# A fused window-attention, global-attention and expert kernel on one core: closing products in the ring of first scores, the last chunk's scores on full columns, token norm sums on GpSimd

## The reference

```
x: [16, 56, 56, 32] f32
x = x + window_attention_block(group_norm(x))   # 7x7 windows, 4 heads, MLP
t = x as tokens                                 # [16, 3136, 32]
n = layer_norm(t)                               # over the 32 channels
q, k, v = n Wq + bq, n Wk + bk, n Wv + bv
t = t + (softmax(q k^T / sqrt(32)) v + n)       # one head, 3136 x 3136 scores per image
n = layer_norm(t)
t = t + experts(n)   # 16 experts: each takes its 8 best tokens of an image, pools
                     # them, two small layers, result added to those tokens
```

## Time and profile before

| | |
|---|---|
| median of 3 runs | 2749.19 us (2747.32 to 2753.39) |
| the profiled execution's own time | 2750.07 us |
| its span, first to last instruction | 2748.3 us |
| TensorE matmuls busy | 2550.2 us, 93% |
| VectorE busy | 2308.6 us, 84% |
| ScalarE busy | 2111.2 us, 77% |
| GpSimd busy | 621.9 us, 23% |
| mean granted TensorE clock | 0.969 of full speed |

### The profile page before, as it was taken

How to read it: one execution, slowest core, us unless ns; L and a number is a source line. 1 busy time by engine, 2 the same in 40 slices (tenths; PEclk the granted TensorE clock), 3 DMA queues, 4 the chain that set the end, 5 groups by cost and what they waited for, 6 DMA issues and landing times.

```text
span 2748.3 us, 118778 instructions
## 1 busy us (share of the span) xinstructions
PE 2550.2 (93%) x54353; PEld 1772.0 (64%) x54353; DVE 2308.6 (84%) x2944; ACT 2111.2 (77%) x3927; POOL 621.9 (23%) x506
## 2 busy tenths in 40 slices
PE   4899999999698999999999999999999999999987
PEld 3455555555343777777777777777777776777756
DVE  5799999999457988889889888898898888988943
ACT  4688888888643888788888887888888877878872
POOL 0566666666400101101101011011010110110100
PEclk6899999999897999999999999999999999999997
DMA  4000000000165010110110101101101011010003
GB/s 103 8 20 26 20 20 25 20 26 20 64 267 124 3 27 3 27 27 3 27 27 4 27 3 27 27 3 27 27 3 27 4 26 27 3 27 3 3 2 95
DMA packets 92807, 85.93 MB, mean 31 GB/s; under 512 B 61108, under 2 KB 82197, under 8 KB 91285
## 3 DMA queue, kind: packets, MB, share of 16 engines
q1 hardware_dynamic: 92085, 78.29, 10.8%
q10 hardware_dynamic: 224, 0.07, 0.0%
HBM read 39.60 MB, written 32.11 MB: 26 GB/s over the span
## 4 chain that ended last, share of the span: by engine, by line
PE 75%; ACT 11%; DVE 8%; issue 4%; SPq 1%; DMA 1%; POOL 0%; POOLq 0%; DVEq 0%; ACTq 0%
PE ps L1711 18%; PE ps L1696 17%; PE ps L1668 16%; ACT arena L911 5%; PE ps L1496 3%; DVE arena L1159 3%; PE ps L1774 2%; DVE arena L1271 2%; PE ps L1515 2%; PE ps L1488 2%; PE ps L1506 2%; PE ps L1527 2%; ACT arena L743 1%; PE ps L1543 1%; PE ps L1566 1%
## 5 line engine op out<-in xcount | busy, mean ns | idle before, releaser
L1271 DVE TENSOR_REDUCE arena<-ps 128x2 f32<-128x896 f32 (+1 forms) x1408 | 1485.8, 1082 | 193.7 <-PE ps L1668 189.4
L911 ACT ACTIVATE arena<-ps 128x512 f32<-128x512 f32 (+1 forms) x2464 | 1351.2, 597 | 310.0 <-PE ps L1696 299.8
L1696 PE MATMUL ps<-arena 97*32 97x512 f16 x10976 | 1104.1, 354 | 11.1 <-issue 6.7
L1711 PE MATMUL ps<-arena 128*32 128x128 f32 x19200 | 1009.3, 273 | 27.9 <-ACT arena L911 19.4
L1668 PE MATMUL ps<-arena 96*32 96x448 f16 x10976 | 885.6, 356 | 18.6 <-DVE arena L1261 8.9
L1711 PEld LDWEIGHTS ps<-arena 128*32 128x32 f32 x19200 | 702.9, 110 | 226.5 <-ACT arena L911 67.3
L1668 PEld LDWEIGHTS ps<-arena 96*32 96x32 f16 x10976 | 381.5, 97 | 178.0 <-DVE arena L1271 85.9
L1696 PEld LDWEIGHTS ps<-arena 97*32 97x32 f16 x10976 | 394.1, 95 | 40.5 <-ACT arena L911 11.5
L640 POOL TENSOR_TENSOR tok<-arena,tok 128x128 f32<-128x128 f32 (+1 forms) x112 | 48.0, 428 | 1359.6 <-DVE arena L1293 1357.7
L585 POOL TENSOR_TENSOR arena<-arena 113x784 f32<-113x784 f32 x128 | 192.7, 1505 | 156.5 <-DVE arena L1135 156.5
L580 POOL TENSOR_TENSOR arena<-arena 113x784 f32<-113x784 f32 x128 | 192.6, 1505 | 86.8 <-DVE arena L1124 86.8
(11 more groups left out here) (188 smaller groups left out, 2457.4 us busy)
## 6 DMA issues: line engine op xcount, KB each, us to landing
arena<-qk_scratch SPq DMA_DIRECT2D x96, 196.0 KB, 4.0
qk_scratch<-arena SPq DMA_DIRECT2D x16, 512.0 KB, 4.4
arena<-ximg SPq DMA_DIRECT2D x16, 400.0 KB, 7.1
arena<-in_x SPq DMA_DIRECT2D x4, 1568.0 KB, 10.9
xa_scratch<-arena SPq DMA_DIRECT2D x32, 196.0 KB, 1.9
res_scratch<-arena SPq DMA_DIRECT2D x32, 196.0 KB, 2.0
arena<-xa_scratch SPq DMA_DIRECT2D x4, 1568.0 KB, 8.3
arena<-res_scratch SPq DMA_DIRECT2D x4, 1568.0 KB, 11.0
```

Source lines behind the costliest of these rows:

```text
L911: act.activation(pk[0:rows, k % DEPTH, QC * m:QC * m + n], ps[0:rows, w % SB, 0:n], ACT.Exp, scale=float(C) ** -0.5).then_inc(att["exp"], 1)
L1271: dve.tensor_reduce(mxp[0:rows, p, 2 * u:2 * u + k], ps[0:rows, at_:at_ + k, 0:KN], AX_X, ALU.max)\
L1696: last = pe.matmul(ps[r:r + 32, bank, at_ % QC:at_ % QC + chunk_cols(c)], k2[p][0:97, T * t + r:T * t + r + 32], q2[p][0:97, QC * c:QC * c ...
L1711: last = pe.matmul(ps[C * g:C * (g + 1), AVB, 0:T], vf[p][:, t, :], pk[:, x % DEPTH, at_ + T * g:at_ + T * (g + 1)], start=(t == 0), stop= ...
```

## The change

Five things are done; the new orders follow from the tables.

1. The closing product no longer writes to bank 3 but takes a slot of the ring of first scores. A table `ring_no` numbers all uses of the ring, pairs and closing products, in TensorE's order; a use waits until the one two before it has been consumed (`ring_free`). VectorE's product of a closing counts `ring` as a maximum does, and VectorE works the slots off in the same order.
2. The first key sums of a chunk wait for ScalarE's copy (`acopy`), and no longer for VectorE. Nothing is held back a step: COPY_LAG is 2, the copy stands between the two exponentials of its step, and the sums of a chunk's first step come behind the closing product. Steps 53 to 56 become

The diff, cut to its core:

```diff
-        SUMS_LAG, COPY_LAG, OUT_LAG, WEIGHTED_LAG = 2, 3, 3, 4
-
-        def sums_step(x):
-
-            return x + SUMS_LAG + int(x in first_of)
+        SUMS_LAG, COPY_LAG, OUT_LAG = 2, 2, 3
 
         def sums_at(k, place):
 
-            found = [(x, late) for late in (1, 0) for x in range(NSTEP) if sums_step(x) - NSTEP * late == k]
-            end, both = scores_of[k], len(found) > 1
-            tiles = [(x, late, i) for x, late in found for i in range(len(steps2[x][1]) if steps2[x][0] < NQ - 1 else 1)]
-            return [m for n, m in enumerate(tiles) if place == (end if both or n else min(1, end))]
+            x, late = (k - SUMS_LAG) % NSTEP, int(k < SUMS_LAG)
+            c, tiles, _ = steps2[x]
+            places = [scores_of[k]] * 2 if x == first_of[c] else [1, scores_of[k]]
+            return [(x, late, i) for i in range(len(tiles) if c < NQ - 1 else 1) if places[i] == place]
+
+        def closings_at(k, place):
+
+            return chunk_ended(k - OUT_LAG) if place == scores_of[k] else []
 
...
+        ring_no = {("first", 0, u): u for u in range(AHEAD)}
+        for b in range(B):
+            for k in range(NSTEP):
+                for place in range(scores_of[k] + 1):
+                    for _, ahead, u in jobs_at(k, place, b == B - 1):
+                        ring_no["first", b + ahead, u] = len(ring_no)
+                    for c, late in closings_at(k, place):
+                        if b >= late:
+                            ring_no["closing", b - late, c] = len(ring_no)
+        for c in (NQ - 2, NQ - 1):
+            ring_no["closing", B - 1, c] = len(ring_no)
...
+        def ring_bank(no):
+
+            return MB + 2 * (no % 2)
...
-                pool.wait_ge(att["o"], b * NQ + c + 1)
+                pool.wait_ge(att["ring"], ring_no["closing", b, c] + 1)
...
+            def channel_sum(v):
+
+                w = C // 2
+                ln_step(pool.tensor_tensor(lnq[:, :, 0:w], v[:, :, 0:w], v[:, :, w:C], ALU.add))
+                while w > 1:
+                    w //= 2
+                    ln_step(pool.tensor_tensor(lnq[:, :, 0:w], lnq[:, :, 0:w], lnq[:, :, w:2 * w], ALU.add))
...
+                channel_sum(tb)
+                ln_step(pool.tensor_scalar(lnv[:, 1, :], lnq[:, :, 0], 1.0 / C, None, ALU.mult))
+                ln_step(pool.tensor_tensor(lnc[:, :, :], tb, per_tile(lnv[:, 1, :]), ALU.subtract))
+                ln_step(pool.tensor_tensor(lnq[:, :, :], lnc[:, :, :], lnc[:, :, :], ALU.mult))
...
+                channel_sum(lnq)
+                ln_step(pool.tensor_scalar(lnv[:, 3, :], lnq[:, :, 0], 1.0 / C, 1e-5, ALU.mult, ALU.add))
+                ln_step(pool.tensor_tensor(lnv[:, 4, :], lnv[:, 3, :], half[:, :], ALU.pow))
+                pool.wait_ge(att[f"load{p}"], b * 56 + 112 - 56 * p)
+                pool.tensor_tensor(xf[:, :, bass.ds(b, 1), :].rearrange("p t o c -> p (t o) c"), lnc[:, :, :],
                                    per_tile(lnv[:, 4, :]), ALU.mult).then_inc(att["xf"], 1)
...
+                if b or c:
+                    act.wait_ge(att["score1"], ring_no["closing", b - (c == 0), (c - 1) % NQ] + 1)
...
-                    for c, late in chunk_ended(k - COPY_LAG):
-                        if not (late and first):
-                            sums_copy(b - late, c)
                     if k >= DEPTH or not first:
                         act.wait_ge(att["av"], b * NSTEP + k - DEPTH + 1)
-                    for w_, m, rows, n, _ in units[k]:
+                    for i, (w_, m, rows, n, _) in enumerate(units[k]):
                         w = place_of(w_, last)
+                        if i:
+                            for c, late in chunk_ended(k - COPY_LAG):
+                                if not (late and first):
+                                    sums_copy(b - late, c)
                         act.wait_ge(att["score2"], b * (NUNIT - NQ) + score_no(w_))
                         act.activation(pk[0:rows, k % DEPTH, QC * m:QC * m + n], ps[0:rows, w % SB, 0:n], ACT.Exp,
...
+                no = ring_no["first", b, u]
+                t, k, at_, done = mine[0] // NK, len(mine), ring_bank(no), no + 1
...
-                o4 = ps[0:rows, AVB, 0:(C + 1) * k].rearrange("p (t n) -> p t n", n=C + 1)
-                dve.wait_ge(att["out"], b * NQ + c + 1)
+                no = ring_no["closing", b, c]
+                o4 = ps[0:rows, ring_bank(no), 0:(C + 1) * k].rearrange("p (t n) -> p t n", n=C + 1)
+                dve.wait_ge(att["score1"], no + 1)
+                if b or c:
+                    dve.wait_ge(att["ring"], ring_no["closing", b - (c == 0), (c - 1) % NQ] + 1)
...
-                dve.tensor_tensor(oa[0:rows, i, 0:k, :], o4[:, :, 0:C], rd, ALU.mult).then_inc(att["o"], 1)
...
+                dve.tensor_tensor(oa[0:rows, i, 0:k, :], o4[:, :, 0:C], rd, ALU.mult).then_inc(att["ring"], 1)
...
-                    for c, late in chunk_ended(k - WEIGHTED_LAG):
-                        if not (late and first):
-                            weighted(b - late, (p + late) % 2, c)
                     for place in range(scores_of[k] + 1):
-                        for j, ahead, u in jobs_at(k, place, last):
-                            consume(b + ahead, (p + ahead) % 2, u, j, b * NJ + AHEAD + j + 1)
-                            if j == LN_AT:
-                                sum_slot(b)
-                            if j == LN_AT + 1:
-                                mean_slot(b)
-                            if j == LN_AT + 9:
-                                square_sum(b)
-                            if j == LN_AT + 10:
-                                variance_slot(b)
+                        for _, ahead, u in jobs_at(k, place, last):
+                            consume(b + ahead, (p + ahead) % 2, u)
+                        for c, late in closings_at(k, place):
+                            if not (late and first):
+                                weighted(b - late, (p + late) % 2, c)
 
...
+            def ring_free(no):
+
+                if no >= 2:
+                    pe.wait_ge(att["ring"], no - 1)
+
+            def produce(b, p, u):
+
+                no = ring_no["first", b, u]
+                ring_free(no)
                 if u == 0:
...
-                    for r in range(0, tile_rows(t), 32):
-                        last = pe.matmul(ps[r:r + 32, bank, at_ % QC:at_ % QC + chunk_cols(c)],
-                                         k2[p][0:97, T * t + r:T * t + r + 32],
-                                         q2[p][0:97, QC * c:QC * c + chunk_cols(c)], start=True, stop=True)
+                    if c < NQ - 1:
+                        for r in range(0, tile_rows(t), 32):
+                            last = pe.matmul(ps[r:r + 32, bank, 0:QC], k2[p][0:97, T * t + r:T * t + r + 32],
+                                             q2[p][0:97, QC * c:QC * c + QC], start=True, stop=True)
+                    else:
+                        last = pe.matmul(ps[:, bank, at_ % QC:at_ % QC + TL], k2[p][0:97, T * t:T * t + T],
...
-                    pe.wait_ge(att["o"], b * NQ + c)
+                    pe.wait_ge(att["acopy"], b * NQ + c)
...
+                no = ring_no["closing", b, c]
+                ring_free(no)
                 pe.wait_ge(att["acopy"], b * NQ + c + 1)
                 n = min(chunk_cols(c), T)
                 w = C + 1 if n < T else 4 * (C + 1)
                 for r in range(0, n, 32):
-                    last = pe.matmul(ps[r:r + 32, AVB, 0:w], ua[:, r:r + 32], wvo[:, :] if n < T else wv4,
+                    last = pe.matmul(ps[r:r + 32, ring_bank(no), 0:w], ua[:, r:r + 32], wvo[:, :] if n < T else wv4,
                                      start=True, stop=True)
-                last.then_inc(att["out"], 1)
+                last.then_inc(att["score1"], 1)
 
...
-                        for j, ahead, u in jobs_at(k, place, last):
-                            produce(b + ahead, (p + ahead) % 2, u, j, b * NJ + AHEAD + j - 1)
-                        if place == scores_of[k]:
-                            for c, late in chunk_ended(k - OUT_LAG):
-                                if not (late and first):
-                                    out_values(b - late, c)
+                        for _, ahead, u in jobs_at(k, place, last):
+                            produce(b + ahead, (p + ahead) % 2, u)
+                        for c, late in closings_at(k, place):
+                            if not (late and first):
+                                out_values(b - late, c)
```

More of the change, by code:

```diff
@@ L267, in conv_attention_moe @@
             "load0", "load1", "score1", "ring", "maxall", "mrow", "score2", "exp",
-            "av", "acopy", "out", "rden", "o", "tok", "sum", "mean", "diff", "square", "ss", "var", "rstd", "xf")}
+            "av", "acopy", "rden", "tok", "ln", "sum", "mean", "diff", "square", "ss", "var", "rstd", "xf")}
         moe = {n: sem("moe_" + n) for n in (
@@ L643, in per_tile @@
```

(41 more changed lines are left out.)

48 lines of the change are left out of this document (27 added, 21 removed).

## The result

| | median of runs (us) | ratio to before |
|---|---|---|
| before | 2749.0 | |
| after | 2708.75 (4 runs, 2706.8 to 2710.5) | 0.9851 [0.9834, 0.9868] |

40.3 us less, where 33 were forecast. The profiled execution went from 2750.07 to 2710.5: 39.6. Of these the 15 periods from one image's end to the next give 33.9 (1650.1 to 1616.3), the last image up to its closing product of chunk 5 gives 3.1, and what stands behind that 3.1; the start gives 0.5 back. A typical image went from 109.5 to 107.5: fifteen times that difference is 30. The other 4 of the 33.9 come from images that ran longer than the typical one, of which there were more before (see the last experiment).

The account below looks back on a forecast made before the run. TensorE's holes at closings and image's end, some 6 of 109.5 us per image, were taken to bound it. Terms -2.6 - 0.6 + 1.4 - 0.3 = -2.1, over 15.5 images -33: 2716 us, own range 2703 to 2730, 8-in-10 range 2692 to 2752.

Parts of the forecast that it names:

- What bounds the kernel: Attention loop: TensorE has 103.5 us of work in an image of 109.5, so some 6 us are holes.
- Closings, -2.6 per image: Five full-chunk closings: closing product in the ring, key sums freed by ScalarE's copy; saves 2.6 us, bounds 1.3 and 3.9.
- VectorE starting 0.61 after P starts: Input on the ring: VectorE's maximum begins 0.61 us after a pair of first scores starts on TensorE.
- the walk: Step-by-step timing of ring slots at a closing: waits of 0.2 us in place of 0.78; reused for the image's end.
- Image's end, -0.6: At the image's end, waits of 1.3 us replace a hole of 1.92, saving 0.6; bounds 0 and -1.9.
- Last chunk on full columns, +1.4: Last chunk's second scores, steps 78 and 79: slower tiles and layout changes cost 1.4 us per image; bounds -0.1 and +4.3.
- the load's growth by a third of a nanosecond a column: Last chunk's weight loads: f16 rows gave 0.35 ns a column, so 60 ns a tile was taken, +0.7 us per image.
- the +1.0: Last chunk: eight column-layout changes around four score units cost 1.0 us per image; bounds 0 and +2.0.
- the 0.3 that was taken off: Last chunk: some 0.3 us of the layout-change cost falls into TensorE's idle time at 1538.17.
- Rival B: Last chunk's full columns cost nothing, neither weight loads nor layout changes: -3.5 us per image, 2695 us; chance 0.15.
- Token norm, -0.3: VectorE loses two reductions of 0.98 us; each leaks 0.16 to TensorE, saving 0.3 per image; bounds 0 and -2.3.
- 15.5 images: Multiplier for the per-image saving: sixteen images, but the first lacks a predecessor's end and the last a successor's scores.

Follow-up runs that it names:

- the last experiment: Last chunk's second scores put back on 32 columns, against the changed kernel with first-score pairs spaced at closings and spread evenly: 2666.78 us, 0.9691 to the kernel before.
- the order with no holes at all: Changed kernel with first-score pairs spaced around closings and the eight extra pairs moved to mid-chunk: 2656.83 us, 0.9661 to the kernel before.
- The part alone: Kernel before with only closing products in the ring and key sums released by ScalarE's copy, issued without delay: 2717.94 us, 0.9885.
- the norm's part alone: Kernel before with the token norm's channel sums on GpSimd as the only change: 2740.57 us, 0.9964.
- four pairs of runs: Kernels differing only in the last chunk's scores, 32 against full columns; shortest images 109.45/109.84, 107.62/108.01, 107.07/107.44 and 103.78/104.15 us.

## Why the prediction was right, and where its terms were not

The direction, the mechanism and the rough size were right; the total came 7 lower than forecast. That a typical image gained 2.0 where 2.1 were forecast is luck: the closings gave half of their term and the last chunk cost a quarter of its own.

- *What bounds the kernel.* Right: the holes, not the work. Even the order with no holes at all leaves 104.2 per image, and the count of work had said 103.5.
- *Closings, -2.6 per image.* The mechanism was right: the burst is gone, K waits for nothing, and OUT and P wait for maxima. The size was not. The part alone gave -1.8 in a typical image with the image's end in it. By the steps of the whole change, with the norm's 0.56 taken out, the image's end gives 0.56 and the five closings 1.24 in place of 2.6, just past the bound of 1.3. The input that failed is "VectorE starting 0.61 after P starts": that was read at the image's end, where a wait had just brought the strips together. At a closing it is 0.78, and the earlier trace rows had the longer P of 0.73 in its first line. The three plain closings then saved 0.33 to 0.35 each (4.34 to 4.01 for chunk 3), not 0.58, and that of chunk 2 as much, where 0.4 was taken. That of chunk 1, taken at -0.5, cost 0.13 to 0.14 (steps 26 to 38 take 17.24 after, 17.11 with the norm's part alone); the walk never went through it.
- *Image's end, -0.6.* Measured -0.53 on TensorE, -0.56 by the steps. OUT waited 0.74, the walk had said 0.77. Here 0.61 was the right input.
- *Last chunk on full columns, +1.4.* Mis-sized: +0.38 (2.74 for 2.36 in steps 78 and 79; 0.37 to 0.39 in the shortest images of four pairs of runs). A tile takes 30 ns, not 60, which is nearly the lower bound of 27, so 25 tiles take 0.75 for the 0.78 before, and the term of +0.7 was nothing. The step that failed is the load's growth by a third of a nanosecond a column. One load of 128 f16 columns is shown as 98 ns, where the earlier trace rows has 95 for 32:

```profile
L1732 PEld LDWEIGHTS ps<-arena 97*128 97x128 f16 x400 | 15.4, 98 | 12.7 <-issue 9.5 <-ACT arena L946 3.2
```

  The Trainium skill, TensorE: Matmul & The Clock Gate, Weight-path perf modes, describes a faster load for 128 non-FP32 weight columns, and the 30 ns agree. The change of layout was sized about right: 0.10 to 0.14 on the way in and 0.10 on the way out, some 0.9 for four units (an estimate from these rows) against the +1.0. But more of it than the 0.3 that was taken off fell into idle time. Before, 0.46 lay between the last unit, two short matmuls, and the S behind it at 1538.17; after it is 0.20. Rival B had the tile right and the layout wrong.
- *Token norm, -0.3.* Measured -0.56 to -0.6. The slack of 0.82 was worked out for the steady rhythm with 0.61 again; with 0.78 it is 0.65, and each reduction of 0.98 leaks 0.33. The runs show 0.28 to 0.31.
- *Sum.* -1.24 - 0.56 + 0.38 - 0.56 = -1.98 by the parts, and a typical image gives -1.99. The mean of the 15 periods is -2.3 (33.9 / 15), since more images ran long before, up to 112.8. No term of the forecast stands for that.
- *Not foreseen: 3.1 at the last image and 3.1 behind it.* "15.5 images" gave the last one half a term. Behind it, before, TensorE idled 0.80 for a copy and 0.72 for the division, and then the clock was lower. In two stretches before the clock was on average 0.88 and 0.68 of full speed; from 2637.5 to 2639, across their border, it was 0.50, the 1.2 GHz level. After, it stayed at the full 2.4 (columns of the earlier trace rows):

```profile
2634.50:2638.00 3.50, 2.07 (x64) 1.59 (x65) 0.76 (x4) 0.57 (x4) 0.46 (x1) 0.88 0.02 7
2638.00:2642.00 4.00, 4.00 (x21) 3.03 (x20) 2.01 (x5) 1.20 (x2) 0.25 (x1) 0.68 0.00 0
```

```profile
2598.00:2600.20 2.20, 1.32 (x62) 1.21 (x62) 0.47 (x2) 0.59 (x4) 0.45 (x1) 1.00 0.03 7
2600.20:2604.20 4.00, 4.00 (x32) 2.81 (x28) 3.00 (x7) 2.07 (x4) 0.24 (x1) 1.00 0.00 0
```

The same sixteen transposes, before and after:

```profile
2637.56 3.41 PE L1823 MATMUL ps<-cst,ximg 128*128 128x128 f32 x16
```

```profile
2600.24 1.97 PE L1861 MATMUL ps<-cst,ximg 128*128 128x128 f32 x16
```

1.4 of the 3.1 is that one line at the lower granted clock.

## What to carry to other kernels

When a product moves into a ring, walk the ring with the consumer's start read at the place itself: a producer group that the timeline shows longer than its siblings hands over later. A ring of two slots whose consumer is busy for over 85% of the time has to be fed at even distances; here evening out the takers was worth more (52 us) than the whole change (40), with the same work and the same memory. Take what was freed for the order that it allows: the same freeing without the new order was slower than before.

## What the hardware showed that was not expected

- A product on one of four column strips seems to leave the strips out of step for the groups behind it: a pair of first scores then spans 0.73 in place of 0.56, and its consumer starts 0.78 in place of 0.61 after it, until a wait aligns them. The lengths are shown, the cause is argued.
- f16 matmuls of 64 moving columns with 128 weight columns run at 30 ns each, new weights every time; a load of 128 f16 columns is shown as 98 ns, one of 32 as 95.
- Eight such tiles between column-tiled work cost 0.10 to 0.14 on the way in and 0.10 on the way out. Of some 0.9 per image about half went into idle time that was there, and 0.38 stayed in every undisturbed image.
- With 98 short matmuls in place of 25, single images ran long more often, in four pairs out of four: in all 7.0 to 18.7 us over 14 images against 1.2 to 5.1. The cause is open.
- Two idle times of 0.8 and 0.7 us at a stage's border went with a granted clock of 0.88 and then 0.68 on average behind them (0.50 from 2637.5 to 2639); with 0.52 and 0.47 there it stayed at 1.00.
